# Graph attention layer on one core: be2 added by GpSimd from an on-chip tile in place of accumulating transfers, and a new order of steps

## What is computed

```python
q, k, v = h @ Wq, h @ Wk, h @ Wv                    # 8 heads of 64
e = einsum('ehd,ehd->eh', k[src], q[dst]) / 8
attn = softmax of e over the edges with one dst
o = segment_sum(attn * v[src], dst) @ Wo            # rows that are no dst get 0
x1 = layernorm(h + o, ln1_g, ln1_b)
f  = relu(x1 @ W1 + b1) @ W2 + b2
x2 = layernorm(x1 + f, ln2_g, ln2_b)
out = layernorm(h + x2)                             # ln2_b is be2 in the kernel
```

## Time and profile before

| | |
|---|---|
| median of 3 runs | 687.24 us (686.03 to 687.55) |
| the profiled execution | 688.38 us, of which 686.0 us is the span of its instructions |
| busy | PE 641.2 us, DVE 579.7, ACT 527.7, POOL 401.5 |
| mean granted TensorE clock | 0.983 |

### The profile page before, as it was taken

One profiled execution on the slowest core, in us unless ns is written; L12 is line 12 of the kernel. 1 busy time (PEld: TensorE's weight loads), 2 busy tenths in 40 slices (PEclk: granted clock), 3 DMA queues, 4 the chain that ended last, 5 costly groups with the idle time before them and its releaser, 6 DMA issues.

```text
span 686.0 us, 10819 instructions
## 1 busy us (share of the span) xinstructions
PE 641.2 (93%) x3498; PEld 486.7 (71%) x3498; DVE 579.7 (85%) x1391; ACT 527.7 (77%) x1140; POOL 401.5 (59%) x363
## 2 busy tenths in 40 slices
PE   3999999999999999999999999999999999989940
PEld 2787877777777777777777777777778778765520
DVE  7648778969998898898889889988998898899692
ACT  2435258996888988898798889888888999698881
POOL 7164363685776865766676677654548826645423
PEclk9999999999999999999999999999999999999985
DMA  7734144546625745584374458245554654554362
GB/s 231 219 95 120 46 122 91 165 111 147 181 61 166 169 134 135 158 175 91 135 178 127 106 159 202 53 156 127 124 134 151 151 92 150 123 107 123 108 117 90
DMA packets 37746, 91.42 MB, mean 133 GB/s; under 512 B 8346, under 2 KB 9642, under 8 KB 37690
## 3 DMA queue, kind: packets, MB, share of 16 engines
q0 software_dynamic: 31536, 82.74, 47.1%
q1 hardware_dynamic: 6154, 8.01, 4.0%
HBM read 71.20 MB, written 20.99 MB: 134 GB/s over the span
## 4 chain that ended last, share of the span: by engine, by line
PE 83%; ACT 6%; DVE 4%; issue 2%; DMA 1%; POOL 1%; SPq 0%; POOLq 0%; DVEq 0%
PE pP L962 63%; PE pF L1102 5%; PE pT L1022 5%; PE pF L1094 5%; PE pT L1058 4%; ACT squares L557 3%; DMA xs<-in_x_dram,src_idx 1%; PE pS L1029 1%; DVE rows L897 1%; ACT rows L617 1%; ACT nT L585 1%; DVE rows L891 1%; ACT sd L549 0%; POOL xs L411 0%; ACT rows L576 0%
## 5 line engine op out<-in xcount | busy, mean ns | idle before, releaser
L557 ACT ACTIVATE squares<-rows,nmean 125x512 bf16<-125x512 f32 x200 | 142.2, 713 | 40.8 <-DVE nmean L901 18.2
L415 POOL DMA_INDIRECT out_dram<-rows,node_idx x40 | 45.5, 1137 | 73.0 <-ACT rows L617 64.2
L411 POOL DMA_INDIRECT x_rows<-in_x_dram,node_idx x40 | 46.7, 1168 | 55.9 <-DVE rows L916 46.5
L472 POOL DMA_DIRECT2D x_rows<-in_L_gnn_ln_b_dram x40 | 53.1, 1405 | 27.1 <-DVE rows L820 21.3
L962 PE MATMUL pP<-wo_hi,aT_hi 128*125 128x512 f32 x160 | 66.4, 415 | 0.5 <-DVE aT_lo L847 0.5
L962 PE MATMUL pP<-xTd_hi,wq_hi 128*128 128x500 f32 x160 | 66.4, 415 | 0.0
L962 PE MATMUL pP<-xTs_hi,wv_hi 128*128 128x500 f32 x160 | 65.6, 410 | 0.0
L897 DVE SCALAR_TENSOR_TENSOR rows<-pF,rows 125x512 f32<-125x512 f32 x78 | 50.6, 686 | 17.2 <-PE pF L1102 16.4
L962 PE MATMUL pP<-xTs_hi,wk_hi 128*128 128x500 f32 x160 | 63.3, 396 | 0.0
L962 PE MATMUL pP<-xTd_lo,wq_hi 128*128 128x500 f32 x160 | 63.1, 394 | 0.0
L962 PE MATMUL pP<-wo_lo,aT_hi 128*125 128x512 f32 x160 | 63.0, 394 | 0.0
(11 more groups left out here) (197 smaller groups left out, 1761.7 us busy)
## 6 DMA issues: line engine op xcount, KB each, us to landing
x_rows<-in_L_gnn_ln_b_dram POOLq DMA_DIRECT2D x40, 512.0 KB, 6.8
dst_row<-in_dst_dram SPq DMA_DIRECT2D x9, 250.5 KB, 3.6
q<-in_L_gnn_Wq_dram SPq DMA_DIRECT2D x1, 1024.0 KB, 5.8
rows<-in_L_gnn_Wk_dram SPq DMA_DIRECT2D x1, 1024.0 KB, 7.9
rows<-in_L_gnn_Wv_dram SPq DMA_DIRECT2D x1, 1024.0 KB, 9.0
x_rows<-in_L_gnn_Wo_dram SPq DMA_DIRECT2D x8, 128.0 KB, 5.0
xd<-in_x_dram,dst_idx POOLq DMA_INDIRECT x40, 4.1
xs<-in_x_dram,src_idx POOLq DMA_INDIRECT x40, 3.7
```

Source lines behind the costliest of these rows:

```text
L411: pool.indirect_dma_start(rows, None, x, bass.IndirectOffsetOnAxis(ap=table[:, column:column + 1].bitcast(U32), axis=0), bounds_check=N - ...
L415: pool.indirect_dma_start(out, bass.IndirectOffsetOnAxis(ap=table[:, column:column + 1].bitcast(U32), axis=0), rows, None, bounds_check=N ...
L472: pool.dma_start(xr_wide[n], bass.AP(tensor=be2.tensor, offset=be2.offset, ap=[[0, P], [0, 2], [1, D]]), accum_op=ALU.add).then_inc(s[f"be ...
L557: ins = act.activation(squares[:, t, :], w[n][:, t, :], ACT.Square, bias=nmean[c][n][:, t:t + 1], accum_out=sq[c][n][:, t:t + 1])
```

## The change

A tile `be2_all` (be2 on every partition) is loaded once by the SyncE queue, behind g1 and g2 and ahead of b2. The step `be` becomes two additions on GpSimd, 125 x 512 floats each, in place. To make room, `weight`, a tile of the softmax, becomes a view of `far`, the mask's tile, which is dead when `weight` is written; two waits guard this (GpSimd's mask waits for `log_taken`, ScalarE's S for `decay_half`). All four tables of the plan are new.

```diff
-PERIOD = 7684
-SLOT_PERIOD = {"N0": 7683, "N1": 7685}
+PERIOD = 7711
+SLOT_PERIOD = {"N0": 7712, "N1": 7708}
 PLAN = {
...
-N0.be 146112 148981 147856 187736 255091; N0.out 149610 152159 152660 240814 379749;
+N0.be 145206 149966 148318 193444 256218; N0.out 154743 152800 152184 245965 408197;
...
+        be2_all = sb("be2_all", [P, D])
...
-        weight = sb("weight", [P, EG])
+        weight = far[:, 0:EG]
...
-            for tile, vec in ((g1_all, g1), (g2_all, g2)):
+            for tile, vec in ((g1_all, g1), (g2_all, g2), (be2_all, be2)):
                 sp.dma_start(tile[:, :], to_all(vec, D)).then_inc(s["all_loaded"], 16)
...
                     on.wait_ge("decay_done", i)
+                    on.wait_ge("log_taken", i)
                     pool.tensor_scalar(far[:, 0:EG], nsame[:, :], FAR, -FAR, ALU.mult, ALU.add).then_inc(s["mask_done"], 1)
...
-                        pool.dma_start(xr_wide[n], bass.AP(tensor=be2.tensor, offset=be2.offset, ap=[[0, P], [0, 2], [1, D]]),
-                                       accum_op=ALU.add).then_inc(s[f"be_added_{slot}"], 16)
+                        on.wait_ge("all_loaded", 48)
+                        for t in range(2):
+                            ins = pool.tensor_tensor(xr[n][:, t, :], xr[n][:, t, :], be2_all[0:R, :], ALU.add)
+                        ins.then_inc(s[f"be_added_{slot}"], 1)
...
                     on.wait_ge("log_taken", i)
+                    on.wait_ge("decay_half", i + 1)
                     act.activation(weight[:, :], ex[:, 1, :], ACT.Exp).then_inc(s["exp_done"], 1)
...
-                        on.wait_ge("all_loaded", 32)
+                        on.wait_ge("all_loaded", 48)
...
-                        on.wait_ge(f"be_added_{slot}", 16 * (i + 1))
+                        on.wait_ge(f"be_added_{slot}", i + 1)
```

More of the change, by code:

```diff
@@ new lines @@
+V3 74218 138175 140400 149171 207966; S 4861 100018 135942 136160 150941; LN 28846 103092 136312 136266 154520;
+XP 33392 110000 136565 136557 155415; N0.sd 133380 144449 144377 151154 267224;
+N0.norm 140578 145023 144520 161980 274727; <N0.T 145533 145209 145752 171930 371199;
+>N0.T9 147430 158405 139775 177955 294273; >N0.F19 137814 145395 136515 136407 295577;
+<N0.seed 146664 147639 146674 175587 236430; <N0.F1 147958 148249 147524 176857 320595;
+N0.sq 149064 149474 149271 210589 345543; N0.sq3 150732 150244 150124 232729 433601;
@@ new lines @@
+<N0.z 151433 150723 151117 259610 442854; N1.sd 86288 140598 141983 145927 183381;
+N1.norm 89680 142485 142473 148644 189491; N1.T 96376 142784 143510 149638 201386;
+N1.seed 69542 142596 142361 151759 210383; N1.F1 108542 143629 143985 153128 226124;
+N1.sq 130251 144985 145526 155659 241412; N1.sq3 145504 147320 146517 168989 294518;
+N1.z 149054 148510 147666 176741 315000; E0.sd 125944 142001 143465 154630 230526;
+<E0.norm 130565 142700 143954 155928 231702; <E0.T 137982 143105 144088 158774 195082;
@@ new lines @@
+>E0.T9 151381 148570 157143 167188 263293; >E0.F19 150191 157408 142093 180661 271718;
+<E0.seed 135533 144237 144324 161648 255335; <E0.F1 140924 144422 144397 162694 235483;
+E0.sq 145114 146599 146435 165661 287032; E0.sq3 147371 148769 147607 179231 330746;
+E0.z 148945 150174 148297 190441 357983; E1.sd 136397 144278 144356 164181 271428;
+<E1.norm 141245 144790 144405 170785 203334; <E1.T 142696 145031 144794 185145 214616;
+>E1.T9 130813 141987 141369 226483 281816; >E1.F19 141537 146732 134049 206251 291750;
@@ new lines @@
+N0.sum 115273 143570 143533 147659 223397; N0.mv 122089 143874 144103 149169 240645;
+N0.r1 130025 144968 144747 149872 242970; N0.xr 145387 145808 145697 192480 271442;
+N0.x2 148066 148984 148137 193614 299914; N0.m2 148142 149102 148369 200195 301312;
+N0.t 148883 149493 148943 208449 370554; N0.r2 148841 149263 148978 209489 349162;
+N0.y 149132 149922 149136 210611 387718; N0.m3 149647 149972 149165 212183 438820;
+N0.r3 150533 150307 150059 225196 447266; >N0.z9 316325 265741 244731 247789 506114;
@@ new lines @@
+N1.sum 69171 137077 140533 142143 175892; N1.mv 74702 137663 140578 146149 180127;
+N1.r1 92689 140094 141994 146763 192359; N1.xr 105049 142040 143330 152288 209832;
+N1.x2 112686 143351 143871 155788 219142; N1.m2 119476 144776 144743 156258 219415;
+N1.t 126171 145300 145350 160363 231647; N1.r2 126638 145439 145352 160210 226734;
+N1.y 129110 145448 145697 161163 249154; N1.m3 133575 146538 145797 169583 261598;
+N1.r3 145832 148109 147120 191713 279936; E0.m1 112412 141327 143125 154775 215411;
```

159 lines of the change are left out of this document (65 added, 94 removed).

## The result

The changed kernel takes **767.59 us** (median of 4 runs, 767.43 to 771.22) against 686.72 of the kernel before on the same chip: a ratio of 1.118, interval 1.1153 to 1.121. The forecast was 689.2 us with a range of 684.6 to 693.4. It was 78 us too low, and the measured time lies outside the range.

A forecast was written before the change was run, and what follows sets the result against it. The prediction took TensorE to bound the middle rounds (61.47 us each) and a chain over VectorE, then ScalarE, the end. Terms 0 + 0 + 0 + 1.7 + 0.3 = +2.0 us on the 687.24 median gave 689.2 us, range 684.6 to 693.4.

The forecast's parts named there:

- VectorE's loss per addition: Wherever GpSimd's additions meet VectorE's two-tile work: 0.34 us lost per addition, bounds 0 to 0.68.
- 5.3 us of two-tile work: VectorE's chain from 653.26 to 658.4 us, slowed at a rate of 0.23 to 0.47: 1.2 to 2.5 us, 1.7 taken.
- GpSimd's 2.0 us per addition: GpSimd's own time for one 125 x 512 addition: 2.0 us taken, bounds 0.60 and 2.9.
- Middle rounds 0: Middle rounds stay at 61.47 us: VectorE's 2.7 us loss fits in its 6.8 us of idle time.
- New order 0 in the middle: Middle rounds: TensorE's list keeps the same steps per round, so its own time stays 61.47 us.
- the rival hoped for 2 us at the end: New order closes 2 us of TensorE's idle time from 600 to 630 us, giving 685.2 us; chance 0.25.
- Removed transfers 0: Whole kernel: the forty transfers are hidden on all sides, so removing them gains 0.
- Shared tile, waits and load 0: Softmax and beginning: new waits are met before, 12 us cover the extra load; cost 0.
- End +2: End: six additions slow VectorE's chain by 1.7 us, pairs of rounds 8 and 9 add 0.3; +2.0 us.
- The last rival: Additions of 2.9 us make GpSimd late in middle rounds and at the end: 692.8 us; chance 0.12.
- the signs of being wrong: Middle round over 61.6 us; TensorE idle 600-630 down over 1 us; 1.2 us additions beside two-tile work; end chain off VectorE.
- the forecast's own range: Whole kernel: 688.6 to 690.6 us, from 1.2 or 2.5 us at the end with the rest; chance 0.33.

The follow-up runs named there:

- e10: Graph attention left out; five VectorE instructions of one form, alone or beside GpSimd operations: two-tile form 3.10 us alone, 5.14 beside two additions, 3.81 beside two one-input operations.
- e17: As e10, with GpSimd's two additions whole or in 2, 4 and 8 pieces each: VectorE loses 2.04, 1.99, 1.16 and 0.49 us.
- e9: Kernel before in its old order, GpSimd additions for the two node slots alone (40 of 80), transfers for the edge slots: 727.55 us, ratio 1.059.
- e5: Changed kernel without the step be and without y's wait for it, so be2 is not added: 692.5 us, ratio 1.0073.
- e15: Kernel before without its be transfers and the waits on them, so be2 is not added: 687.80 us, ratio 1.0001.
- e1: Changed kernel with be again one accumulating transfer per slot; new order, shared tile, load and new waits kept: 701.54 us, ratio 1.020.
- e7: Kernel before, old order and transfers, plus the shared tile, its two waits and the load of be2: 687.58 us, ratio 1.000.
- e18: Kernel before in its old order with GpSimd's additions, each cut in four pieces of 128 columns: 748.17 us, ratio 1.0895.
- e4: Changed kernel with each addition over 256 of 512 columns, half of be2 left out: 706.72 us, ratio 1.028.
- e6: Changed kernel with every addition cut in four pieces of 128 columns: 724.64 us, ratio 1.053.
- e8: Same kernel as e15, on a slower chip where the kernel before takes 698.2 us: 712.57 us, ratio 1.0208.
- e14: Same kernel as e16, on the slow chip: 736.53 us, ratio 1.0548.
- e16: Kernel before in its old order, VectorE adding be2 itself in 40 instructions of 125x1024, GpSimd doing nothing for be2: 723.48 us, ratio 1.0521.

## Why the prediction was wrong, step by step

The step that failed is the price of an addition on VectorE, and with it the zero for the middle rounds. Most of the loss is not at the end, where the forecast put all of it: when the last round's first scan starts, the kernel is already 66.2 us behind (658.91 against 592.73), and only 13.6 us are added after it.

- **VectorE's loss per addition: 0.34 us taken, 0 to 0.68 as bounds; measured 1.06 in the kernel, 1.02 by itself.** This is the term that failed. It was read off, where the mask takes 1.48 us and L891 1.56 beside it, and doubled as the bound for the second input. e10 suggests another reading: the mask is a 0.60 us operation that waited for VectorE's, and L891's 0.34 us are the hold of one such operation (0.36 in e10). The forecast counted one loss for two mask operations; VectorE's next row in the kernel before shows the second, 0.33 us more than the 1.41 of the earlier trace rows:

```profile
367.12 1.74 DVE L906 SCALAR_TENSOR_TENSOR rows<-rows,nmean,g_all 125x512 f32<-125x512 f32 x2
```

What had to be scaled was the operation's own length, 0.60 us for the mask and 1.26 for an addition. VectorE then loses nearly all of it (1.02 in e10, 0.94 beside the form with a scalar) or somewhat more (1.34 and 1.35 per addition for L814 and L907). The forecast read two engines that slow each other; e10 and e17 look like two engines that exclude each other.
- **Which instructions pay.** L897 of before was rightly called safe. That the two-tile lines were the only ones to pay was wrong: a TENSOR_SCALAR of two columns pays the same (2.02 us for two additions in e10), and up to 5.2 us in the kernel. "5.3 us of two-tile work" at the end times a rate was the wrong form of sum; nearer is the number of additions times about 1 us wherever one such instruction is due. From 727 to 739 us the six additions cost VectorE 6.1 us, where the forecast had 1.7.
- **GpSimd's 2.0 us per addition (0.60 to 2.9)**: 1.33 measured, inside the bounds. "Meets VectorE, so it is slow" is true only in dense two-tile stretches (1.55 in the last block); elsewhere VectorE is the one that waits.
- **Middle rounds 0, covered by 6.8 us of VectorE's idle time.** Wrong twice. At 1.02 eight additions take 8.2 us, above the 6.8; measured are 9.7 (64.41 against 54.67). And four additions, well below, still cost 3.0 us a round (e9). VectorE's longest idle time stands where it waits for TensorE; a hold can fall where ScalarE or TensorE waits for VectorE, as at 382.64, and TensorE, without any idle time in the earlier trace rows, cannot make it up. That a round also pays in clock (0.53 after the wait of 4.60 us) was in no term.
- **New order 0 in the middle; the rival hoped for 2 us at the end.** The middle was right (61.70 in e5 against 61.47). The end is 4 us longer, not shorter.
- **Removed transfers 0**: shown in the old order (e15). In the new one they cost 9 us (e1, e5), in which `y` waits for a landing three times, 12.25 us in all.
- **Shared tile, waits and load 0**: shown (e7, ratio 1.000).
- **End +2.** From the last round's first scan (658.91) to the end of the span it is 106.9 us against 93.3, so +13.6, of which the order without be is 4.1. The block of six was expected from 652 to 664 us with 2.0 us each; its additions took 1.55.
- **The last rival**, slower by GpSimd's lateness from 2.3 us per addition, had the sign but not the mechanism: GpSimd's 40.4 us in a round of 70.6 is no bound.
- Of the signs of being wrong that the prediction names, two came: additions of about 1.25 us beside a two-tile instruction (L814) and a middle round far beyond 61.6 us.
- **A slip in the sums.** With 1.2 or 2.5 us at the end and 0.3 for the rest, the forecast's own range on 687.24 is 688.7 to 690.0, not 688.6 to 690.6. Nothing hangs on it.

The Trainium skill has a rule that would have given the price of an addition. "SBUF — State Buffer", section "SBUF: two separate sides", says that VectorE and GpSimd share one pair of ports under an exclusive lock, held for the whole instruction, and that the one that comes second fully blocks. e10 agrees in the length (2.04 us for two additions). Whether the one that comes second is the one that blocks, the rows do not settle: at 454.34 and 412.91 the held VectorE instruction is shown as started first, and at 240.84 in e18 one is held through many GpSimd instructions, on which the sentence says nothing. By that rule and GpSimd's length the sum in the middle would have been eight times 1 us against 6.8 of cover, a loss. For what the two engines do to each other the forecast used only the Trainium skill's "GPSIMD Engine Reference", section 8, which calls it contention, and let the trace's one-input row put a size on it. The Trainium skill's "VectorE: DVE Perf Modes", section "Mode 2×_2P — use both read ports for one tensor", bears on the tiny instructions: a one-input operation can take both read ports. e10's TENSOR_SCALAR, 0.35 us for 512 floats where other forms take 0.62, and its 2 us of loss agree.

## What to carry to other kernels

Before moving element-wise work to GpSimd, count it as VectorE time: about the operation's own length on GpSimd (here 1.0 to 1.3 us for 1.26), each time VectorE has a two-tile or TENSOR_SCALAR instruction due, however small. Doing it on VectorE can be the cheaper of the two (here 0.61 us per 512 columns against 1.02). And an engine's idle time covers an addition to its work only where nobody waits for what comes next. Here four additions a round cost VectorE 4.8 us and the round 3.0, though VectorE kept 5.0 us of idle time (e9).

## What the runs showed of the hardware

- Back-to-back additions can hold one VectorE instruction for the whole block: 6.04 us for a 0.67 us one, 5.34 us for a 125x2 one, 9.30 us beside a block of 24 pieces (e18). In a dense row of two-tile instructions the engines took turns instead (after, from 726.85 us; e10 and e17). What decides between the two is open.
- A VectorE instruction with an input in a product bank, and bn_stats, were not held (3.08 and 3.07 us in all three columns of e10; L903 at most 0.693 us in 78).
- GpSimd's two-input addition has a fixed part: at its shortest 1.25 us for 512 columns, 0.72 for 256 (e4), 0.44 for 128 (e6).
- After TensorE had waited 4.60 us its granted clock was 0.53 for the next 3.60 us, and 1.00 again in the 5 us after 395.00.
- Chips differ: the kernel before takes 698.2 us on one (7 runs) and 686.7 to 687.9 on the others. Without be the old order's second round takes 73.6 us there and 68.8 elsewhere (e8, e15), and the two kernels that ran on both of them, e8/e15 and e14/e16, lose 25 and 13 us.
